# Statistics on ScalarE, 13 input products on GpSimd, a column-grouped product for B and C, smaller ScalarE jobs in a Mamba and expert layer

## The reference

```python
x = x + mamba(layernorm(x)); x = x + ffn(layernorm(x))
# mamba: rmsnorm, @W_in -> (xs, res), causal conv of 4 taps and silu on xs,
#   xs @ W_x -> (dt, B, C), dt = softplus(dt @ W_dt),
#   h[d,n] = exp(-exp(A_log)[d,n] * dt[d]) * h[d,n] + dt[d] * B[n] * xs[d]   (512 channels d, 16 states n)
#   y[d] = sum_n h[d,n] * C[n];  out = xn + (y * silu(res)) @ W_out
# ffn: 8 experts, each for its own 512 tokens: (silu(x @ w1) * (x @ w3)) @ w2, 704 hidden
```

## Time and profile before

| | |
|---|---|
| median of 3 runs | 985.3 us (985.3 to 986.16) |
| profiled execution, device time | 985.27 us |
| its span | 983.5 us |
| TensorE busy | 913.5 us (93%) |
| VectorE busy | 900.4 us (92%) |
| GpSimd busy | 892.1 us (91%) |
| ScalarE busy | 732.3 us (74%) |
| granted TensorE clock, mean | 0.983 of 2.4 GHz |

### The profile page before, as it was taken

The page is one execution under the profiler, slowest core; times in us unless marked ns, Lnnn a source line. Parts: engine busy times, 40 slices in busy tenths (PEclk is TensorE's granted clock), DMA queues, the critical chain, the costliest instruction groups (busy, mean ns, idle before and its releaser), DMA issues.

```text
span 983.5 us, 13018 instructions
## 1 busy us (share of the span) xinstructions
PE 913.5 (93%) x4172; PEld 594.7 (60%) x4172; DVE 900.4 (92%) x966; ACT 732.3 (74%) x1305; POOL 892.1 (91%) x425
## 2 busy tenths in 40 slices
PE   6989989999999999999999999999999998769898
PEld 4545455655765576755856566754766556745765
DVE  5889899899999999999999999999999989999951
ACT  4667877978778878888779877888788785567630
POOL 1498899999999999999999999999999999999920
PEclk9999999999999999999999999999999999779899
DMA  5580154012642049021651038120580027200110
GB/s 175 222 298 22 43 215 173 29 40 100 260 157 67 1 171 343 4 68 59 233 225 43 25 103 340 76 68 12 190 315 21 27 95 277 102 22 3 59 50 21
DMA packets 43476, 116.82 MB, mean 119 GB/s; under 512 B 8592, under 2 KB 27024, under 8 KB 34192
## 3 DMA queue, kind: packets, MB, share of 16 engines
q1 hardware_dynamic: 41552, 115.94, 32.2%
q10 hardware_dynamic: 1856, 0.04, 0.1%
HBM read 110.21 MB, written 5.77 MB: 118 GB/s over the span
## 4 chain that ended last, share of the span: by engine, by line
PE 36%; DVE 36%; ACT 15%; issue 11%; DMA 1%; POOL 0%; DVEq 0%; SPq 0%; ACTq 0%; POOLq 0%
DVE ring L658 25%; PE gbank L1091 19%; DVE ring L643 9%; PE ybank L1154 7%; PE gbank L1105 6%; ACT ebank L787 4%; ACT hb L1020 2%; ACT sres L868 1%; ACT xs L864 1%; ACT L1016 1%; PE gbank L1099 1%; ACT L876 1%; ACT L872 1%; DMA hb<-in_L_attn_W_x_dram 1%; PE gbank L1225 1%
## 5 line engine op out<-in xcount | busy, mean ns | idle before, releaser
L658 DVE TENSOR_TENSOR_SCAN ring<-ebank,state,ring 128x512 f32<-128x512 f32 x512 | 623.7, 1267 | 28.8 <-ACT ebank L787 21.6
L516 POOL TENSOR_TENSOR hc<-ring,c_all 128x1024 f32<-128x1024 f32 x255 | 600.8, 2381 | 14.0 <-DVE ring L658 6.4
L787 ACT ACTIVATE ebank<-dt_,a_neg 128x512 f32<-128x512 f32 x512 | 347.2, 689 | 165.0 <-DVE ring L658 162.5
L1154 PEld LDWEIGHTS ybank<-ident,hc 128*128 128x128 f32 x2048 | 237.8, 144 | 106.5 <-issue 52.0
L1154 PE MATMUL ybank<-ident,hc 128*128 128x128 f32 x2048 | 265.2, 278 | 31.9 <-POOL hc L516 23.2
L502 POOL TENSOR_TENSOR ring<-b_all,u 128x1024 f32<-128x1024 f32 x109 | 259.5, 2381 | 9.9 <-DVE taken L607 9.5
L643 DVE TENSOR_TENSOR ring<-b_all,ubank 128x1024 f32<-128x1024 f32 x145 | 173.4, 1196 | 0.0
L1091 PE MATMUL gbank<-xT,w 128*128 128x512 f32 x320 | 148.1, 597 | 15.2 <-DVE hb L738 12.4
L1091 PE MATMUL gbank<-xT,w_a 128*128 128x512 f32 x256 | 119.1, 602 | 8.3 <-DVE dt_ L632 4.4
L1091 PEld LDWEIGHTS gbank<-xT,w 128*128 128x128 f32 x320 | 57.3, 190 | 82.2 <-issue 56.7
L1091 PE MATMUL gbank<-xs,w_a 128*128 128x512 f32 x224 | 100.8, 593 | 0.7 <-ACT sres L805 0.7
(11 more groups left out here) (146 smaller groups left out, 750.9 us busy)
## 6 DMA issues: line engine op xcount, KB each, us to landing
b_all<-bc_kept SPq DMA_DIRECT2D x32, 1024.0 KB, 6.7
c_all<-bc_kept SPq DMA_DIRECT2D x32, 1024.0 KB, 8.4
w<-in_L_ffn_w_dram SPq DMA_DIRECT2D x16, 640.0 KB, 4.9
w_a<-in_L_attn_W_in_dram SPq DMA_DIRECT2D x7, 1024.0 KB, 4.9
w_a<-wc_kept SPq DMA_DIRECT2D x7, 1024.0 KB, 4.8
w2s<-in_L_ffn_w_dram SPq DMA_DIRECT2D x8, 640.0 KB, 9.4
xin<-in_L_attn_x_dram SPq DMA_DIRECT2D x9, 512.0 KB, 3.6
x<-in_L_attn_x_dram SPq DMA_DIRECT2D x7, 512.0 KB, 6.4
```

Of the source, the lines that this page charges most:

```text
L516: ch_ok.by(e.tensor_tensor(hc[:, q % HC, :, :], ring[:, q % RING, :, :], c_all[:, n:n + NG, :], ALU.mult))
L658: h_ok.by(e.tensor_tensor_scan(row, ebank[j % 2][:, :], row, initial=state[:, q, n:n + 1], op0=ALU.mult, op1=ALU.add))
L787: e_ok.by(e.activation(ebank[j % 2][:, :], dt_[:, d, :], ACT.Exp, scale=a_neg[:, d, k:k + 1]))
L1154: last = e.matmul(ybank[:, cols(b)], hc[:, q % HC, n, cols(b)], ident[:, :], is_transpose=True, start=(k == 0 and n == 0 and b == 0), stop ...
```

## The change

The statistics of x move from VectorE's `x_stats` to ScalarE, as eight passes with an accumulated output (a sum, then a sum of squares around the mean, for each of four blocks of 128 tokens) with the first half of `u` as a scratch target; the input product of tile 21 moves from GpSimd to VectorE in chunks 1 to 7; the product for B and C is made as four groups of 32 output rows, each for 128 of the 512 tokens, and leaves through `yt`; and several of ScalarE's jobs are cut or moved. Setup, which makes the statistics of chunks 0 and 1, keeps `x_stats`.

```diff
-    POOL_BU = (1, 4, 7, 10, 11, 14, 17, 18, 21, 22, 23, 24, 27, 29)
+    POOL_BU = (1, 4, 7, 10, 11, 14, 17, 18, 22, 23, 24, 27, 29)
+        bc_b = yt[:, 0:P]
+        BC_AFTER = (1, 0)
+        sums = Event("sums", NT)
 # SyncE
-                    e.dma_start(bc_kept[:, :], bc_s).then_inc(bc_out.sem, 16)
+                    e.dma_start(bc_kept[:, :].rearrange("m (b t) -> b m t", b=NT), bc_b).then_inc(bc_out.sem, 16)
 # GpSimd
-            table = [..., (21, "next", front), ...]          # table0: 23
+            table = [..., (24, "next", front), ...]          # table0: 26
 # VectorE
-                     (19, "next", x_stats), (19, "scan", gated(1)), (20, "back", hidden(0)), (20, "back", hidden(1)),
-                     (20, "back", hidden_tail), (21, "back", hidden(2)), (22, "back", hidden(3)), (23, "back", hidden(4)),
+                     (20, "scan", gated(1)), (20, "back", hidden(0)), (20, "back", hidden(1)),
+                     (20, "back", hidden_tail), (20, "back", hidden(2)), (21, "back", hidden(3)), (22, "back", hidden(4)),
 # ScalarE
+            def x_sums(*bs):
+                def job(c, i):
+                    x_in.wait(e, c)
+                    bup_ok.wait(e, i, before(pool_bu(i), 2 * GPD))
+                    for b in bs:
+                        sums.by(e.activation(u[:, b // 2, b % 2 * D:(b % 2 + 1) * D], xin[:, b, :], ACT.Copy, accum_out=mv[:, b, 0:1]))
+            def x_mean(c, i):
+                sums.wait(e, c - 2)
+                roots.by(e.activation(st[:, c % 3, 2, :], mv[:, :, 0], ACT.Copy, scale=-1.0 / D))
+            def x_squares(*bs):
+                def job(c, i):
+                    roots.wait(e, c, 1)
+                    for b in bs:
+                        last = e.activation(u[:, b // 2, ...], xin[:, b, :], ACT.Square, bias=st[:, c % 3, 2, b:b + 1], accum_out=mv[:, b, 1:2])
             def rooted(c, i):
+                of = 1.0 if c < 2 else 1.0 / D               # folded into the two Ln
+                if c < 2:
+                    roots.by(e.activation(mine[:, 2, :], mv[:, :, 0], ACT.Copy, scale=-1.0))
             def bc_read(c, i):
-                bc_out.wait(e, c - 1)
+                    wait_full(e, i, "YT", BC_AFTER[i > 0])
+                    read_out(e.activation(bc_b, bank[:, 0:P], ACT.Copy), i, "BC", 0)
             def y_read(d):
+                    if has_front(i) and d == BC_AFTER[i > 0] + 1:
+                        bc_out.wait(e, c + 1)
             def gate_silus(c, i):
                 e.preload_act_table(ACT.Silu)
-                if has_front(i):
-                    res_silu(c + 2, i)
                 ...
                 silu_ok.by(e.activation(hb[FR:P, FT, :], hb[FR:P, FT, :], ACT.Silu))
+                if has_front(i):
+                    res_silu(c + 2, i)
-  table: (0, before_conv(0, 1)), (2, before_conv(2, 3)), (17, gate(0, 1)), (22, rooted), (29, normal)
+  table: (0, before_conv(0)), (1, before_conv(1)), (2, before_conv(2)), (3, before_conv(3)), (17, gate(0, 1)),
+         (17, x_sums(0, 1)), (20, gate_silus), (21, x_sums(2, 3)), (21, x_mean), (22, x_squares(0, 1)),
+         (23, x_squares(2, 3)), (24, rooted), (28, normal_rows(0, 1)), (29, normal_rows(2, 3))
+  table0: (23, x_sums(0, 1)), (24, x_sums(2, 3)), (25, x_mean), (25, x_squares(0, 1)), (26, x_squares(2, 3)), (26, rooted)
 # TensorE, bc
-                filled(product(bank[0:W, :], [(wbc[:, k, :], xs[:, k, :]) for k in range(ND)]), i, "BC", 0)
+                for k in range(ND):
+                    for b in range(NT):
+                        last = e.matmul(bank[b * W:(b + 1) * W, 0:P], wbc[:, k, :], xs[:, k, cols(b)], start=(k == 0), stop=(k == ND - 1),
+                                        skip_group_check=True)
+                filled(last, i, "BC", 0)
```

More of the change, by code:

```diff
@@ L532, in _ @@
                     bu(0, q)
-            table = [(4, "scan", u_of(ND - 1)), (10, "back", back), (21, "next", front), (24, "front", u_of(0)),
+            table = [(4, "scan", u_of(ND - 1)), (10, "back", back), (24, "next", front), (24, "front", u_of(0)),
                      (27, "front", u_of(1)), (29, "front", u_of(2))]
-            table0 = [(3, "late", u_of(1)), (7, "late", u_of(2)), (10, "late", u_of(3)), (23, "next", front),
+            table0 = [(3, "late", u_of(1)), (7, "late", u_of(2)), (10, "late", u_of(3)), (26, "next", front),
                       (27, "front", u_of(0)), (28, "front", u_of(1)), (29, "front", u_of(2))]
@@ L762, in _ @@
             table0 = [(0, "late", fed), (4, "late", dt_of(1)), (5, "late", dt_of(2)), (9, "late", dt_of(3)),
[L763 removed]
+                      (19, "scan", gated(0)), (23, "scan", gated(1)), (27, "front", dt_of(0)),
                       (27, "front", dt_of(1)), (29, "front", dt_of(2)), (30, "scan", gated(2)), (30, "front", dt_of(ND - 1))]
@@ L819, in rooted, with normal_rows, job @@
                 roots.by(e.activation(mine[:, 5, :], mine[:, 7, :], ACT.Identity, bias=1.0))
[L821 to L825, removed]
+            def normal_rows(*bs):
+                def job(c, i):
+                    scales.wait(e, c)
+                    for b in bs:
+                        xn_ok.by(e.activation(xin[:, b, :], xin[:, b, :], ACT.Identity,
+                                              bias=st[:, c % 3, 3, b:b + 1], scale=st[:, c % 3, 4, b:b + 1]))
+                return job
+            normal = normal_rows(*range(NT))
             def turned(name):
@@ L1079, in _ @@
                       (18, "front", convolved(1)), (18, "front", convolved(2)), (19, "front", convolved(3)),
-                      (19, "front", silus_first), (20, "scan", y_read(1)), (20, "front", res(0, 1)), (22, "front", res(2, 3)),
-                      (24, "front", bc_read), (25, "next", rooted), (25, "front", softplus(0)), (27, "front", softplus(1)),
+                      (19, "front", silus_first), (20, "scan", y_read(1)), (20, "front", res(0, 1)), (22, "front", res(2, 3)), (23, "next", x_sums(0, 1)),
+                      (24, "front", bc_read), (24, "next", x_sums(2, 3)), (25, "next", x_mean), (25, "next", x_squares(0, 1)), (26, "next", x_squares(2, 3)),
+                      (26, "next", rooted), (25, "front", softplus(0)), (27, "front", softplus(1)),
                       (27, "scan", y_read(2)), (28, "next", normal), (29, "front", softplus(2)), (30, "front", softplus(ND - 1)),
```

28 lines of the change are left out of this document (18 added, 10 removed).

## The result

The changed kernel takes 991.66 us (median of four runs, 990.64 to 991.91) beside 985.65 for the kernel before: ratio 1.0055, interval [1.0043, 1.0067]. It is slower by 0.55%; the forecast was 981.3, with a range that ended at 988.5. The profiled execution took 990.64 us, its span is 988.8, its mean granted clock 0.974 (before: 0.983).

The account below looks back on a forecast made before the run. A loop through GpSimd, TensorE and ScalarE was taken to set the 113.19 us period; -0.5 in five iterations (-2.5), -0.9 in iteration 1 and -0.55 in the tail made -3.95, 985.27 to 981.3, range 975 to 988.5.

Parts of the forecast that it names:

- B: Grouped product for B and C on TensorE, with its readout and DMA: 3.5 down to 0.9 us, no gain.
- S: Statistics moved to ScalarE: nothing gained on VectorE's shadowed work, 0.45 per accumulating pass, stalls of 0.95 on VectorE's path.
- P: 13 products, tile 21's input product moved from GpSimd to VectorE: 0 in steady iterations, -0.55 in the tail.
- J: before_conv in four and normal in two on ScalarE: VectorE's waits of 0.90 and 0.46 go.
- H: Gate's Silu first, hidden(2) and gated(1) at tile 20: VectorE loses waits of 0.55 and 0.6, TensorE 1.8, per iteration.
- no gain, cover 0.42: Product for B and C: TensorE spends time saved waiting for tile 12; its existing 0.42 wait there covers a loss.
- Rival 4: Each weight load stands open before its B and C product, 6.9 us in all: slower, 994, chance 0.05.
- sum 0.95 on VectorE's own path: Stalls from ScalarE's statistics: 0.35 at scan 18, 0.1 at tile 23, 0.5 at scan 25.
- 1.94 of gains: VectorE's savings per iteration: 0.90 at scan 1, 0.46 before scan 30, 0.6 for hidden(2).
- the loop: GpSimd tiles 21 to 12, TensorE to TAIL, ScalarE's Silu block and scans: sets the 113.19 period, can fall to 112.67.
- -0.46 and -0.90: VectorE's waits before scan 30 and at scan 1, expected to go when normal and before_conv are split.
- The 0.6 of hidden(2): VectorE's hidden(2) moves into the shadow of ScalarE's Silu block, saving 0.6 per iteration.

Follow-up runs that it names:

- u_bc_stats_pool: Changed kernel without grouped B and C product, ScalarE statistics and 13 products, leaving only the smaller or moved ScalarE jobs and earlier gate Silu: 981.85 us, ratio 0.9958.
- u_bc_pool: Changed kernel with the old B and C product and tile 21's input product back on GpSimd, statistics still on ScalarE: 987.20 us, ratio 1.0008.
- u_bc: Changed kernel with the old product for B and C, its readout and its DMA: 987.41 us, ratio 1.0011.
- p_bc3: Changed kernel with the grouped product for B and C made three times over, new readout and DMA kept: 987.39 us, ratio 1.0010.
- u_stats_pool: Changed kernel with statistics back on VectorE and tile 21's input product back on GpSimd, grouped B and C product kept: 986.16 us, ratio 0.9999.
- u_bc_stats: Changed kernel with the old B and C product and statistics back on VectorE, 13 products on GpSimd kept: 987.18 us, ratio 1.0010.
- p_bc: Kernel before with only the grouped product for B and C, its readout and its DMA: 990.84 us, ratio 1.0046.
- s_root: u_bc_pool with rooted moved from tile 24 to 26 and GpSimd's front from tile 24 to 25: 983.04 us, ratio 0.9971.
- s_both: s_root with the first sums also moved from tile 17 to tile 19: 982.44 us, ratio 0.9965.
- c_conv_norm: Kernel before with only before_conv cut in four (tiles 0 to 3) and normal in two (tiles 28, 29): 982.64 us, ratio 0.9960.
- c_silu_hid: Kernel before with only the gate's Silu ahead of that of sres, and hidden(2) and gated(1) at tile 20: 986.13 us, ratio 0.9999.
- u_pool: Changed kernel with the input product of tile 21 back on GpSimd (14 products): 990.71 us, ratio 1.0042.
- s_both13: s_both with 13 products on GpSimd, as in the change: 983.47 us, ratio 0.9969.
- c_conv: Kernel before with only before_conv cut in four, one at each of tiles 0 to 3: 982.64 us, ratio 0.9966.

## Why the prediction was wrong

**The balance.** From u_bc_stats_pool (981.85): plus B 4.3, plus S 5.35, plus P beside S 0.2 makes 991.7, for 991.66 measured. The sum closes of itself, as each term is the difference of two of these runs (u_bc_pool, u_bc, the changed kernel). What bears it out is that B has about the same price in three other places (4.3 by p_bc3, 4.6 alone, 4.3 in u_stats_pool). S and P do not add: S first and P 0.2 behind it, or P first at 5.3 (u_bc_stats) and S 0.2 behind it, is the same 5.6, and either one taken out of the changed kernel alone gives 1.0 at most. The forecast was -3.95 for all together, with B at 0 and 0.55 of it from P in the tail; J and H gave -4.4, and the other three took 9.8.

**B, "no gain, cover 0.42": the step that failed most.** Its duration was right (0.9 forecast, 1.08), and the readout, the new waits and the DMA cost nothing (p_bc3). I read the wait for tile 12 as the end of the matter: time saved turns into idle time, so 0. Idle time of TensorE has a price here, since the granted clock may fall behind it: 4.3 to 4.6 us, by u_bc, p_bc3, p_bc and u_stats_pool. None of my rivals had it, though the trace of the kernel before shows a fall behind a wait (at 72.65, above). In iteration 0, which I put at 0, TensorE's wait for `sres` went from 0.7 to 3.20 and the kernel was 2.43 late at the first table load. Rival 4, open weight loads, is refuted by the 1.08 us for 32 products, where it has 6.9: they take 0.3 of the 3.62 in which the same columns went through before, so four column groups do run side by side, as the Trainium skill (TensorEngine Tiling (Array Packing), "Key Properties") has it, by which different tiles load and multiply in parallel.

**S, "sum 0.95 on VectorE's own path": the size was right, what it was set against was not.** The passes cost 0.40 and 0.49 from start to start, for 0.45. The stalls came where I put them: 0.30 and more for 0.35 at scan 18, 0.73 more than without S for 0.5 at scan 25 (1.16 for the 0.43 of u_bc_stats_pool), 0 at tiles 21 and 22. But I set them against 1.94 of gains and let the loop hide the rest. s_root and s_both show that it is the place of two of ScalarE's jobs that costs: rooted at 24 4.2 us; the 0.6 for the sums at 17 and the last 0.6 of the 5.35 are within what the intervals allow, though the period goes from 112.5 to 112.37 with the sums.

**J, "-0.46 and -0.90": 1.36 counted, 0.8 there.** Between scans 25 and 6 VectorE's path has a second one beside it, through `y_read(2)` (the wait of 0.78 shown above) and TensorE to CV and ScalarE's convolved(2). That one had 0.8 of slack before; when the waits go, scan 6 waits. So VectorE's own path was not 113.19 - 1.94 + 0.95 = 112.2 but 113.19 - 0.8 + 0.9 = 113.3, and that is the period of u_bc_pool (113.32 to 113.34, four times) and the first and fourth of the changed kernel (113.31, 113.32).

**The loop, "of 113.19 it can lose 0.52, and nothing else".** The loop was not what bound the kernel: J alone, which moves no job of its legs, brings the period to 112.4. In c_conv_norm GpSimd's leg is 81.94 for 82.26 and TensorE's to TAIL 17.66 for 18.07; the idle times of 0.20 and 0.32 are gone and 0.2 more, half of it where the products before and behind the 0.32 now run in one row. These idle times stood in the loop because VectorE was late. That its legs add up to the period was no proof that it leads: they must, as the first starts one period before the last ends. Its waits of 0.52 spoke against it; they belonged to another path with the same period. No kernel here has a period below 112.3; that the loop is what bounds it there is not shown.

**H.** The earlier Silu of the gate shortens TensorE's wait for hidden(0) at UP 2 (0.80 in c_silu_hid for 1.79 before); alone H is worth 0.1 per period and 0 in the time, with J 0.8 at most (981.85 for 982.64, whose intervals overlap). The 0.6 of hidden(2), the third term of my 1.94, is not there.

**P.** "Worth 0 in the steady iterations" holds beside S but for the one period of 113.68, and so does "wait about 2 us for the scan of tile 21" (2.46). Its room, though, is S: with bn_stats in place P costs 5.3 us, 1 of it a fall of the clock (u_bc_stats). The tail, forecast at -0.55, came out at +0.95: tile 21 and hidden(2) together put scan 21 at 7.7 behind the last load, for 6.4, and TensorE's DOWN follows. u_pool (without P) and s_both13 (with it, beside s_both) show it from both sides, 1.0 and 1.1, the second with a fall of the clock in it.

**What stays open.** Iterations 2, 3, 5 and 6 of the changed kernel have the same two waits of TensorE, 0.87 and 1.2, as iteration 4, at full clock (iteration 1 has 1.27 and 1.20). What decides in which of them the clock falls was not tried. Every kernel was traced once, so how often the clock falls in the other runs is known only by their mean clock.

## What to carry to other kernels

Before a product is made shorter, look at what TensorE does next: if it waits, the gain is nothing, and the added idle time can cost the clock of the products behind it; making the short product several times tells this cause from a readout or a DMA that came with it. A wait can be filled for nothing only where it stands: the same 3.5 us of ScalarE's work cost 5.3 us with two of its jobs at tiles 17 and 24, and nothing that the times show with them at 19 and 26. When several paths have the same period, take one wait away before you believe which of them leads. The fastest version measured is u_bc_stats_pool, 981.85 us for 986.22 (ratio 0.9958), the smaller jobs and the earlier Silu without the other three parts; s_both, c_conv and c_conv_norm lie 0.6 to 0.8 above it, within the intervals.

## What the hardware did that I had not expected

- Thirty-two products of 128 columns into four groups of 32 output rows take 1.08 us, ninety-six 2.83, where eight of 512 take 3.62.
- A fall of the granted clock behind idle times of 1.2 to 3.2 us costs 0.9 to 1.4 us each in the changed kernel's trace, and the period grows by it (114.27 for 113.32).
- A pass of ScalarE with an accumulated output is two instructions, 0.40 us (a copy) or 0.49 (a square) and a readout of 0.19, but the next pass starts 0.40 and 0.49 behind the one before, so the readout adds nothing to a row of passes.
